# Two attention layers of a graph network: GpSimd's gathers written out, ScalarE's staging of indices dropped

## The chip, the cores and the metric

One NeuronCore of a Trainium2 chip runs the whole program. Its engines are TensorE (PE in the profile; its weight loads are PEld), VectorE (DVE), ScalarE (ACT), GpSimd (POOL) and SyncE (SP). The metric is the time of one execution on the device in microseconds (us). All tensors of a layer that don't fit on the chip lie in HBM.

## What is computed

Four layers of a graph network over 3,125 nodes with 128 features and 100,000 edges, each behind a layer norm and a ReLU, each added to its input. The two that matter here weigh edges by a softmax over the edges of a node:

```python
# layer 1: graph attention, 8 heads of 16
h = (x @ W).reshape(n, H, C)
e = leaky_relu(a_src[src] + a_dst[dst], 0.2)          # one score an edge and head
alpha = softmax of e over the edges with the same dst
out = segment_sum(h[src] * alpha, dst) + bias
...
# layer 3: queries of the sources against keys of the targets
scores = einsum('ehd,ehd->eh', q[src], k[tgt]) / 4
scores = (scores + edges @ We + be) * cons[tgt] + relu(distances @ Wd1 + bd1) @ Wd2 + bd2
weights = softmax of scores over the edges with the same tgt
out = segment_sum(weights * v[tgt], tgt) @ Wo + bo
```

Layer 0 is a polynomial of the graph's Laplacian, layer 2 three relational convolutions; the change doesn't touch them.

## The kernel before

The edges are sorted by target and dealt out to 816 tiles of 128 edges. `src_i` on the chip holds for every tile one column of 128 source numbers (one per partition). Both attention layers run the same function, `edge_rows`, over the tiles: G = 4 tiles are a group, R = 4 groups a step, so 204 groups in 51 steps. `R` is also the number of slots in each ring of buffers.

For group n, in slot r = n mod 4, five engines work side by side, each through its own instruction stream, tied together by semaphores:

- ScalarE (`scalar`) copies four columns of `src_i` into `st[:, slot, :]`, three groups ahead, once VectorE has consumed group n - 1 (line 2095 waits, line 2097 copies). In layer 3 it then picks 16 numbers for each tile of the next group (line 3203); in both layers it does the factors of a running sum once a step (lines 2429 to 2458), in layer 1 it also keeps blocks of pair sums (line 1947).
- GpSimd (`gpsimd`, line 2023) loops over the 51 steps. For each slot it waits for the staged indices, in layer 1 also for SyncE's store of the slot's last rows, and issues four indirect DMAs, the gathers (line 2031): tile g of the slot gets from HBM the rows of its 128 sources, 136 numbers a row in layer 1, 128 in layer 3.
- SyncE loads, 4 groups ahead, the targets' places within their window (line 2168), in layer 1 stores the gathered rows to HBM (line 2172) and once a step the results of the running sum (line 2464).
- VectorE makes one-hots from the places (line 2041), three groups ahead, and consumes group n (`consume`: layer 1 lines 2843 and 2844, layer 3 lines 3153 to 3167). The last instruction of `consume` raises `s_done`, which starts at R. In layer 3 VectorE multiplies the gathered rows by the keys and sums by head. In layer 1 it makes one-hots of the pair sums between (lines 1917 and 1919).
- TensorE turns one-hots into the targets' rows (line 2131) and, in layer 1, makes pair sums (line 1929).

Every engine's loop holds more than one group: VectorE's, ScalarE's and TensorE's hold two steps in layer 3 and more in layer 1, GpSimd's one step with 16 gathers. Nothing but the semaphores orders the engines among themselves; the order on each is the order of the code. Another stage, the first sort of the edges, issues 784 indirect DMAs from GpSimd (line 402, rows of 16 bytes, from the chip to HBM) that stand written out one behind the other.

## Time and profile before

| | us |
|---|---|
| median of 3 runs | 7,225.01 (7,213.89 to 7,237.66) |
| the profiled execution | 7,228.69 |
| its span, first to last instruction | 7,226.9 |
| layer 1's gathers, first to last | 2,421.4 to 3,777.9 |
| layer 3's gathers, first to last | 5,781.7 to 7,106.4 |

The profile has one line for each instruction that an engine executed, with its start, its duration, the idle time before it and what ended that idle time. Waits, branches and register instructions are not counted as busy; "issue" as a releaser means that the profile shows nothing that the engine waited for. Names leave out numbers: `l_edges_by_src` is the ring of gathered rows of either layer, and one can tell the layers apart by the source, `l_by_src` in layer 1 and `l_q` in layer 3. `l_edges_st` are the staged indices.

### The profile page before, as it was taken

What the parts mean: (1) busy time and instruction counts of PE and PEld (TensorE: products, weight loads), DVE (VectorE), ACT (ScalarE), POOL (GpSimd) and SP (SyncE); (2) the same over time, 40 slices, a digit from 0 to 9 for tenths busy, and PEclk for the clock granted to TensorE, in tenths of its full rate; (3) what the DMA queues carried; (4) which work ended last, traced back from release to release, by engine and by line L of the source; (5) the groups of instructions that cost most, each with busy time, mean ns of one, the idle gap of its engine ahead of it and who ended that gap; (6) DMA issues with size and microseconds to landing.
All of it is one profiled execution on the core that took longest, in us unless ns stands there. A gap on an engine that the chain in (4) does not pass through costs nothing. (4 is left out here: it accounts for less than half of the span.)

```text
span 7226.9 us, 87751 instructions
## 1 busy us (share of the span) xinstructions
PE 4193.4 (58%) x18024; PEld 2737.2 (38%) x18027; DVE 3135.0 (43%) x8308; ACT 917.6 (13%) x2931; POOL 3255.4 (45%) x3301
## 2 busy tenths in 40 slices
PE   6820111177799566667765658888888633333333
PEld 6700000022599333333334544444444322222232
DVE  6900111187796555545546761121121344444445
ACT  2100000011100121211210000010010022222221
POOL 0077777600000355555551005646546355555553
PEclk6555555588899787887777989898898855555555
DMA  4300000023477466666663546675665632222232
GB/s 125 94 2 13 8 2 2 10 64 100 156 257 262 126 170 164 168 167 165 172 169 86 145 136 230 216 245 204 213 238 204 198 73 66 69 68 68 67 68 55
DMA packets 564861, 910.88 MB, mean 126 GB/s; under 512 B 100563, under 2 KB 402664, under 8 KB 526004
## 3 DMA queue, kind: packets, MB, share of 16 engines
q1 hardware_dynamic: 459630, 742.44, 32.2%
q0 software_dynamic: 105024, 166.00, 10.1%
q8 instruction: 92, 1.51, 0.1%
q14 instruction: 115, 0.94, 0.0%
HBM read 677.34 MB, written 230.78 MB: 126 GB/s over the span
## 5 line engine op out<-in xcount | busy, mean ns | idle before, releaser
L2031 POOL DMA_INDIRECT l_edges_by_src<-l_by_src,l_edges_st x816 | 795.7, 975 | 1567.3 <-ACT l_edges_st L2080 1005.5
L3027 POOL DMA_INDIRECT l_gathered<-l_table,l_st x816 | 778.1, 954 | 1018.9 <-issue 829.2
L402 POOL DMA_INDIRECT by_src<-src_rec,src_pos x784 | 833.5, 1063 | 530.3 <-DVEq L315 290.6
L2031 POOL DMA_INDIRECT l_edges_by_src<-l_q,l_edges_st x816 | 781.9, 958 | 636.0 <-ACT l_edges_st L2097 300.0
L3096 PE MATMUL psum<-l_blocks,l_rows 128*128 128x512 f32 (+1 forms) x2016 | 891.2, 588 | 68.4 <-issue 65.4
L2131 PE MATMUL psum<-l_rows,l_edges_hot_t 128*128 x1632 | 423.7, 436 | 844.4 <-DVE l_scores L3167 533.3
L1929 PE MATMUL psum<-pair_hot_weight,pair_hot_dst 128*128 128x512 f32 x1200 | 719.3, 741 | 279.5 <-DVE pair_hot_dst L1919 181.8
L2131 PEld LDWEIGHTS psum<-l_rows,l_edges_hot_t 128*128 128x128 f32 x1632 | 360.9, 315 | 914.7 <-issue 914.6
L1163 PE MATMUL psum<-hot_block,hot_low_src 128*128 128x400 bf16 x1136 | 337.7, 420 | 594.6 <-issue 370.7
L3055 DVE TENSOR_SCALAR l_hot<-iota,l_loc,l_weight 128x128 f32<-128x128 f32 x816 | 224.1, 356 | 1051.7 <-DMA pair_blocks<-pair_block 222.4
L1135 DVE TENSOR_SCALAR hot_block<-block_iota,visit_key 128x400 bf16<-128x400 f16 x1136 | 281.3, 319 | 817.5 <-remote 357.4
L3096 PEld LDWEIGHTS psum<-l_blocks,l_rows 128*128 128x128 f32 x2016 | 385.6, 209 | 451.4 <-issue 446.5
L1929 PEld LDWEIGHTS psum<-pair_hot_weight,pair_hot_dst 128*128 128x128 f32 x1200 | 257.8, 233 | 570.8 <-issue 567.8
L1163 PEld LDWEIGHTS psum<-hot_block,hot_low_src 128*128 128x128 bf16 x1136 | 122.3, 108 | 814.5 <-issue 738.7
L2777 PE MATMUL psum<-l_scaled,l_counts 128*128 128x128 f32 x3750 | 425.7, 277 | 1.8 <-ACT l_scaled L2701 1.8
L2777 PEld LDWEIGHTS psum<-l_scaled,l_counts 128*128 128x128 f32 x3750 | 425.0, 194 | 1.9 <-issue 1.9
L1917 DVE TENSOR_SCALAR pair_hot_weight<-pair_iota,pair_staged 128x512 f32<-128x512 f32 x600 | 333.2, 555 | 159.6 <-PE psum L1929 60.2
L3107 PE MATMUL psum<-l_hot,l_gathered 128*128 128x128 f32 x1632 | 263.2, 305 | 163.9 <-issue 149.2
L2131 PEld LDWEIGHTS psum<-l_dst_rows,l_edges_hot_t 128*128 128x128 f32 x1632 | 244.1, 213 | 271.0 <-issue 270.4
L3107 PEld LDWEIGHTS psum<-l_hot,l_gathered 128*128 128x128 f32 x1632 | 241.7, 214 | 271.4 <-issue 271.2
L1626 PE MATMUL psum<-l_sum_rows,l_sum_hot 128*128 128x128 f32 x1632 | 251.0, 302 | 137.6 <-issue 123.9
L2131 PE MATMUL psum<-l_dst_rows,l_edges_hot_t 128*128 x1632 | 235.1, 272 | 132.3 <-issue 107.3
(563 smaller groups left out, 5288.8 us busy)
## 6 DMA issues: line engine op xcount, KB each, us to landing
l_blocks<-pair_blocks SPq DMA_DIRECT2D x216, 1024.0 KB
l_counts<-counts SPq DMA_DIRECT2D x67, 1600.0 KB, 7.0
pair_blocks<-pair_block SPq DMA_DIRECT2D x75, 1024.0 KB
l_edges_loc<-loc_by_tile SPq DMA_DIRECT2D x416, 128.0 KB
l_rows<-l_edges_by_src SPq DMA_DIRECT2D x204, 256.0 KB
l_sum_rows<-l_rows SPq DMA_DIRECT2D x204, 256.0 KB
counts<-count_rows SPq DMA_DIRECT2D x25, 1600.0 KB
attr_space<-in_edge_attr SPq DMA_DIRECT2D x14, 1568.0 KB
```

Source lines behind the costliest of these rows:

```text
L402: pool.indirect_dma_start(table, bass.IndirectOffsetOnAxis(ap=pos[:, e:e + 1], axis=0), rec[:, e, :], None).then_inc(s_out[g % R], 16)
L1135: v.tensor_scalar(self.hot_aj[:, h, n, :], self.at_aj[:, :, :].rearrange("p a j -> p (a j)"), self.key[:, bass.ds(m * TURN + (h * BATCH + ...
L1163: ins = pe.matmul(k.psum[:, bass.ds(bank * PSUM_BANK, AJ)], self.hot_s[:, h, n, :], self.hot_aj[:, h, n, :], start=False, stop=False)
L1626: ins = pe.matmul(k.psum[:, bass.ds(to[g] * D, D)], hot[:, r, g, :], rows[:, r, g, :], start=False, stop=False)
L1917: v.tensor_scalar(self.hot_w[:, place, :], self.wide[:, :], self.near[:, q, j, 1:2], self.near[:, q, j, 2:3], ALU.is_equal, ALU.mult).then ...
L1929: pe.matmul(self.bank(b), self.hot_d[:, place, :], self.hot_w[:, place, :], start=j == self.first[b], stop=j + 1 == self.first[b + 1]).the ...
L2031: pool.indirect_dma_start(a[:, r, g, :], None, table_src, bass.IndirectOffsetOnAxis(ap=st[:, r, g:g + 1], axis=0))\
L2131: ins = pe.matmul(by_place[:, q, g, 0:cols_dst], hot_t[:, r, g, :], by_dst[:, bass.ds(of[g], 1), :].rearrange("p a c -> p (a c)"), start=T ...
L2777: ins = pe.matmul(k.psum[:, to * D:(to + 1) * D], cnt[:, u, to * P:(to + 1) * P], scaled[:, r % 2, w, :], start=n == 0 and to == bank[0], ...
L3027: pool.indirect_dma_start(sent[:, p, g, :], None, by_type, bass.IndirectOffsetOnAxis(ap=st[:, p, g:g + 1], axis=0))\
L3096: ins = pe.matmul(k.ps[c][:, 0:n * P].rearrange("p (a s) -> p a s", s=P), rows[:, b, t * D:(t + 1) * D], blocks[:, 0:n, t, :], start=b == ...
L3107: ins = pe.matmul(k.psum[:, bass.ds(to[g] * P, P)], sent[:, p, g, :], hot[:, p, g, :], start=False, stop=False)
```

## The change

GpSimd's loop is replaced by 204 groups written out one behind the other. Each gather names its own column of `src_i`; the first R groups wait for nothing, and each later one waits for `s_done` to reach n + 1, which says that the group four back, the slot's last, has been consumed. In layer 1 the wait for the stored rows stays. The ring `st`, its semaphores and ScalarE's copies and the waits before them are gone.

```diff
-        st = k.sb(ctx, f"{tag}_st", [P, R, G], I32)
...
         def gpsimd(pool):
-            with pool.Fori(0, steps) as i:
-                for r in range(R):
-                    pool.wait_ge(s_st[r], i + 1)
+            for n in range(T // G):
+                i, r = divmod(n, R)
+                if i > 0:
+                    pool.wait_ge(s_done, n + 1)
                     if keep_rows is not None:
                         pool.wait_ge(s_kept[r], i * 16 + 1)
-                    pool.nop(nofuse=True)
-                    for g in range(G):
-                        pool.indirect_dma_start(a[:, r, g, :], None, table_src,
-                                                bass.IndirectOffsetOnAxis(ap=st[:, r, g:g + 1], axis=0))\
-                            .then_inc(s_row[r], 16)
+                for g in range(G):
+                    pool.indirect_dma_start(a[:, r, g, :], None, table_src,
+                                            bass.IndirectOffsetOnAxis(ap=k.src_i[:, n * G + g:n * G + g + 1], axis=0))\
+                        .then_inc(s_row[r], 16)
...
         def scalar(act):
-            for r in range(R - 1):
-                act.copy(st[:, r, :], k.src_i[:, r * G:(r + 1) * G]).then_inc(s_st[r], 1)
...
             def group(n, r, i, par, pair):
-                ahead = (r + R - 1) % R
...
-                act.wait_ge(s_done, n + R)
-                act.nop(nofuse=True)
-                act.copy(st[:, ahead, :], k.src_i[:, bass.ds((n + R - 1) * G, G)]).then_inc(s_st[ahead], 1)
```

GpSimd in layer 3, the whole loop before. The semaphores bear the names of their first users, since they are used again from stage to stage; here they are the four of the staged indices.

```order
L2024 UNCONDITIONAL_BRANCH
L2024 ISA
L2031 DMA l3_edges_by_src<-l3_q,l3_edges_st 128x128 [waits sort_low_v]
L2031 DMA l3_edges_by_src<-l3_q,l3_edges_st 128x128 x3
L2031 DMA l3_edges_by_src<-l3_q,l3_edges_st 128x128 [waits sort_low_one_set]
L2031 DMA l3_edges_by_src<-l3_q,l3_edges_st 128x128 x3
L2031 DMA l3_edges_by_src<-l3_q,l3_edges_st 128x128 [waits sort_low_counted]
L2031 DMA l3_edges_by_src<-l3_q,l3_edges_st 128x128 x3
L2031 DMA l3_edges_by_src<-l3_q,l3_edges_st 128x128 [waits sort_low_summed]
L2031 DMA l3_edges_by_src<-l3_q,l3_edges_st 128x128 x3
```

The same place after: the first 16 gathers, then the beginning of the 200 groups that follow. Here the semaphore is `s_done`.

```order
L2030 DMA l3_edges_by_src<-l3_q,src_i 128x128 x16
L2030 DMA l3_edges_by_src<-l3_q,src_i 128x128 [waits sort_dist_loaded]
L2030 DMA l3_edges_by_src<-l3_q,src_i 128x128 x3
L2030 DMA l3_edges_by_src<-l3_q,src_i 128x128 [waits sort_dist_loaded]
L2030 DMA l3_edges_by_src<-l3_q,src_i 128x128 x3
L2030 DMA l3_edges_by_src<-l3_q,src_i 128x128 [waits sort_dist_loaded]
L2030 DMA l3_edges_by_src<-l3_q,src_i 128x128 x3
```

The loop and its control instructions are gone, the wait has moved from ScalarE's semaphores to VectorE's, and 16 gathers have become 816 in the stream.

ScalarE in layer 3, from the last copy of a group's terms on, before (layer 3's first group in the loop):

```order
L3203 COPY l3_terms<-l3_terms_by_tile 128x16
L2095 REGISTER_ALU
L2097 ISA [waits sort_dist_loaded]
L2097 COPY l3_edges_st<-src_i 128x4
L2454 REGISTER_ALU
L2455 ISA [waits l1_score_steps]
L2458 COPY l3_run<-psum 128x16x8 [waits l1_turned_turned]
L2458 COPY l3_run<-psum 128x16x8
```

and after:

```order
L3196 COPY l3_terms<-l3_terms_by_tile 128x16
L2447 REGISTER_ALU
L2448 ISA [waits l1_score_steps]
L2451 COPY l3_run<-psum 128x16x8 [waits l1_turned_turned]
L2451 COPY l3_run<-psum 128x16x8
L2087 REGISTER_ALU
```

Between the picked terms and the copies of the running sum a register instruction, the wait for `s_done` and the staging copy are gone; this repeats in every group.

## Rows read from the trace of the kernel before

**Rows 1.** Busy time by stage, layers 1 and 3: stretch, length, busy us (instructions) of PE, PEld, DVE, ACT, POOL; clock, DMA.
```profile
2420.00:3790.00 1370.00, 944.14 (x3042) 512.12 (x3042) 686.63 (x2242) 269.74 (x804) 795.74 (x816) 0.78 0.61 166
5780.00:7110.00 1330.00, 462.89 (x1818) 389.02 (x1818) 563.54 (x1516) 302.80 (x1288) 781.87 (x816) 0.54 0.29 68
```

**Rows 2.** The page's groups: GpSimd's gathers of the two loops: busy, mean ns, idle before.
```profile
L2031 POOL DMA_INDIRECT l_edges_by_src<-l_by_src,l_edges_st x816 | 795.7, 975 | 1567.3 <-ACT l_edges_st L2080 1005.5
...
L2031 POOL DMA_INDIRECT l_edges_by_src<-l_q,l_edges_st x816 | 781.9, 958 | 636.0 <-ACT l_edges_st L2097 300.0
```

**Rows 3.** Waits in layer 1's loop: us in total, times, longest.
```profile
POOL l_edges_by_src L2031 <- ACT l_edges_st L2097: 317.9, 91, 6.4
```

**Rows 4.** Waits in layer 3's loop.
```profile
POOL l_edges_by_src L2031 <- ACT l_edges_st L2097: 300.0, 66, 7.5
...
DVE l_scores L3164 <- ACT l_terms L3203: 15.4, 6, 3.5
```

**Rows 5.** The gathers' line: durations, first and last start; then who waited for them.
```profile
L2031 POOL DMA_INDIRECT l_edges_by_src<-l_by_src,l_edges_st x816: 939/947/1275, 2421.4 to 3777.9; - x164
L2031 POOL DMA_INDIRECT l_edges_by_src<-l_q,l_edges_st x816: 941/947/1242, 5781.7 to 7106.4; - x164
...
who waited for it (us, times):
  DVE l_edges_by_src L3153: 3.2, 1
  DVE dst_f L2843: 1.5, 1
```

**Rows 6.** Timeline of GpSimd in layer 3: start, us, what, idle before and its releaser.
```profile
6379.10 0.95 POOL L2031 DMA_INDIRECT l_edges_by_src<-l_q,l_edges_st  x1 [2.74 <-ACT l_edges_st L2097]
...
6393.10 0.94 POOL L2031 DMA_INDIRECT l_edges_by_src<-l_q,l_edges_st  x1 [0.30 <-issue]
6395.17 0.94 POOL L2031 DMA_INDIRECT l_edges_by_src<-l_q,l_edges_st  x1 [1.12 <-issue]
...
6406.55 0.95 POOL L2031 DMA_INDIRECT l_edges_by_src<-l_q,l_edges_st  x1 [6.68 <-ACT l_edges_st L2097]
...
6420.53 0.94 POOL L2031 DMA_INDIRECT l_edges_by_src<-l_q,l_edges_st  x1 [0.30 <-issue]
6424.77 0.99 POOL L2031 DMA_INDIRECT l_edges_by_src<-l_q,l_edges_st  x1 [3.30 <-ACT l_edges_st L2097]
...
6444.12 0.95 POOL L2031 DMA_INDIRECT l_edges_by_src<-l_q,l_edges_st  x1 [4.58 <-ACT l_edges_st L2097]
```

**Rows 7.** Timeline of VectorE there: the last three instructions of groups.
```profile
6405.24 0.19 DVE L3167 TENSOR_TENSOR l_scores<-l_scores,l_terms 128x32 f32<-128x32 f32 x1
...
6410.31 0.19 DVE L3160 SCALAR_TENSOR_TENSOR l_scores<-l_scores,l_terms 128x32 f32<-128x32 f32 x1 [0.20 <-DVE l_scores L3156]
6410.61 0.19 DVE L3164 TENSOR_TENSOR l_scores<-l_scores,psum 128x32 f32<-128x32 f32 x1
6410.90 0.19 DVE L3167 TENSOR_TENSOR l_scores<-l_scores,l_terms 128x32 f32<-128x32 f32 x1
...
6416.70 0.19 DVE L3160 SCALAR_TENSOR_TENSOR l_scores<-l_scores,l_terms 128x32 f32<-128x32 f32 x1 [1.99 <-issue]
6418.83 0.19 DVE L3164 TENSOR_TENSOR l_scores<-l_scores,psum 128x32 f32<-128x32 f32 x1 [1.94 <-ACT l_terms L3203]
6421.66 0.19 DVE L3167 TENSOR_TENSOR l_scores<-l_scores,l_terms 128x32 f32<-128x32 f32 x1 [2.64 <-issue]
```

**Rows 8.** Timeline of ScalarE there: two staging copies.
```profile
6405.61 0.19 ACT L2097 COPY l_edges_st<-src_i 128x4 int32 x1 [1.43 <-DVE l_scores L3167]
...
6423.83 0.19 ACT L2097 COPY l_edges_st<-src_i 128x4 int32 x1 [2.66 <-issue]
```

**Rows 9.** Written-out scatters of an earlier stage, by stretch: length, POOL busy (instructions), clock, DMA.
```profile
400.00:600.00 200.00, 151.90 (x159) 0.50 0.03 2
...
900.00:1300.00 400.00, 312.88 (x286) 0.50 0.02 2
```

**Rows 10.** Timeline of TensorE's weight loads in that stage.
```profile
906.98 0.10 PEld L1163 LDWEIGHTS psum<-hot_block,hot_low_src 128*128 128x128 bf16 x1 [1.29 <-issue]
908.38 0.10 PEld L1163 LDWEIGHTS psum<-hot_block,hot_low_src 128*128 128x128 bf16 x1 [1.29 <-issue]
```

More of the change, by code:

```diff
@@ L1992, in edge_rows @@
         s_hot, s_mm, s_done = (k.sem(f"{tag}_{name}") for name in ("hot", "by_dst_made", "consumed"))
-        s_st, s_loc, s_kept = ([k.sem(f"{tag}_{name}{r}") for r in range(R)] for name in ("staged", "loc_loaded", "kept"))
+        s_loc, s_kept = ([k.sem(f"{tag}_{name}{r}") for r in range(R)] for name in ("loc_loaded", "kept"))
         s_row = k.pool_dma_sems(f"{tag}_gathered")
```

## The prediction

> **What bounds the kernel now.** I read four views in turn. First the busy time by stage [rows 1]: the edge loops of the two attention layers take some 1,360 and 1,325 of the 7,226.9 us of the span, and nothing else is touched. In the second, GpSimd is the busiest engine (781.87 us of 1,330); in the first TensorE is (944.14 of 1,370).
>
> Then the waits of GpSimd [rows 2 to 4]: it stood idle before its gathers for 317.9 us in 91 waits in layer 1 and for 300.0 us in 66 waits in layer 3, each ended by ScalarE's copy of four index columns. At first sight those 618 us are the prize. A gather takes 958 ns and its successor starts 0.30 us behind it, so 816 of them fill 1,027 of the 1,325 us.
>
> Third, who waits for the gathers [rows 5]: one instruction of VectorE in each layer, 3.2 and 1.5 us. The gathered rows are there long before they are used, in all 204 groups of a layer but these two. So a gather that starts earlier brings nothing by itself. What is late is the consumer.
>
> Fourth, the timelines show why the consumer is late. GpSimd's gathers come in unbroken runs [rows 6]: 12 from 6379.10, 4 from 6395.17, 12 from 6406.55, 12 from 6424.77. VectorE's last three instructions of a group start 0.30 us apart at 6410.3, but 2.1 and 2.8 us apart at 6416.7, although each still takes 0.19 us [rows 7]. ScalarE is slowed at the same time: its staging copy ends 0.4 us behind VectorE's consumption at 6405.43, but 2.2 us behind the one at 6421.85 [rows 7, 8]. Such a slow stretch begins about 5 us into a run and ends some 2 us behind its last gather: in it a group takes VectorE about 10.8 us (6411.1 to 6421.9) where three quick ones took 2.8 us each. I read this as: **while gathers have run unbroken for some 5 us, every other engine gets its instructions only slowly**. The loop's time is the time of gathering, in which the others crawl, plus the pauses of GpSimd, in which they catch up. What causes the slowness no row says, but it decides this change.
>
> **The change, part by part.**
> (1) ScalarE loses, for each group, a wait, one or two register instructions and the copy (0.19 us). That is 204 copies a layer, 39 us of an engine that is busy 303 us of 1,330 [rows 1, 8]. It also loses its tie to VectorE: the picking of layer 3's terms for the next group no longer stands behind a wait for the last group's consumption. VectorE's longest waits for these terms add up to 15.4 us, 6 times [rows 4], so I cost this at nothing; VectorE's own stream and, in layer 1, TensorE's cover it. If that cover were gone it would be a gain of some us.
> (2) GpSimd waits for VectorE's count itself. The ring condition is the same one (the group four back is consumed), only the relay is gone. A quick wait becomes 0.37 us shorter, a wait at the end of a slow stretch 2.2 us. By [rows 5] this is worth nothing on the path. It can't cost the wait itself: the wait sits on the first gather of a group as before, and only gathers queue behind it. In layer 1 the wait for SyncE's store of the slot stays as it was.
> (3) GpSimd's loop of 16 gathers becomes 816 instructions in a row. The loop's branch is taken while earlier gathers still run, so nothing is saved there: the spacing is the same 0.30 us inside and between turns. Whether a written-out gather is as quick as one in a loop is not shown for these loops, but another stage of this kernel has 784 of them written out [rows 9]. Between 400 and 600 us, when the rest is nearly idle, 159 fit in 200 us: 1.258 us each, the price in the loop. Between 900 and 1,300 us, with TensorE and VectorE in their loops, 286 fit in 400 us: **1.399 us each**. In that stretch TensorE's weight loads come 1.40 us apart, though each takes 0.10 us [rows 10], so it is the same slow condition. In the loops of the edge stages a gather keeps its pace in slow stretches too (in the run from 6406.55 the last of 12 starts 13.98 us behind the first, 1.27 us each) [rows 6]. The difference I take for the price of standing outside a loop while others are running.
>
> The bounds of that price: below, nothing (1.258 us as at 400 to 600); above, 1.399 us for all gathers. I take 1.399 for the gathers in slow stretches, since [rows 9] show it over 286 of them, and the present spacing for the others. In layer 3 that is 8 of the 12 of a run (all from 5 us on): 816 x 2/3 x (1.399 - 1.258) = 77 us. In layer 1 GpSimd waits more often (91 times against 66, so 9 gathers to a wait against 12) and its mean gather is 975 ns already (with 0.30 us between, 1.278) [rows 2]; I take a half: 816 x 1/2 x (1.399 - 1.278) = 49 us. Together gathering lasts **126 us longer**.
>
> What of it reaches the end? In added slow time the others do a quarter of the work of quick time (2.8 us against 10.8 us for a group), so three quarters are lost: **95 us**. GpSimd's pauses, some 300 us in each layer, would hide the longer gathering if they were slack; by the fourth view they aren't, because the others catch up in them.
> The sum, against the profiled execution (7,228.7 us, span 7,226.9): 7,228.7 + 95 = 7,324. The median of the runs is 3.7 us below that execution, so 7,320.
>
> The Trainium skill has a rule that speaks the other way ("Runtime: NRT & Kernel Launch", section "Instruction fetch mechanics"): engines stream their instructions in order ahead of use, a block's edge is mostly hidden, and a taken branch out of the window is what stalls, so kernels prefer to be written out. By it part (3) is free and the sum is 7,225. The trace agrees at 400 to 600 us (1.258 us) and disagrees at 900 to 1,300 (1.399 us).
>
> **The rivals.**
> *No change, 7,225.* Written-out gathers keep 1.25 us, say because the 1.399 us belongs to that stage's 16-byte scatters to HBM and not to their form. Then only earlier starts are left, which nobody waits for. For it: [rows 5], the 1.258 us, and the rule above. Against it: the same scatters ran at both prices, and what differed was whether others ran.
> *Faster, about 7,150.* The relay is on the path after all: each of the 157 waits gives back 0.37 us (58 us), and those at the end of a slow stretch 2.2 us; with a sixth of them of that kind, 157 x 1/6 x 1.8 = 47 us more, and a few us each from ScalarE's shorter stream, if the slow stretches are shorter for having fewer instructions in them. About 75 to 110 us. Against it: the rows wait ready for the consumer.
> *Slower by another way, 7,290 or, on top of the forecast, 7,380.* In layer 3 the pause is what lets the others recover, and a pause of 1.1 us does not do it: behind the one at 6394.04 the slow stretch went on. The pause before 6424.77 is 3.3 us now. It would be 1.1 us after the change, because VectorE was done at 6421.85. The turn with the short pause takes 27.45 us for 4 groups (6379.10 to 6406.55), 6.86 a group; the two with long pauses 37.57 us for 6 groups (6406.55 to 6444.12), 6.26. If half the groups of layer 3 go over to the first kind: 102 x 0.6 = 61 us. It decides where the pauses shrink below some 2 us.
>
> **How the numbers follow.** Forecast (gathers slowed by their form, 7,270 to 7,390): 0.40. Shrunken pauses, alone or on top: 0.15. No change: 0.22. Faster: 0.23. A measurement of this kernel can tell about 0.3%, 22 us, from no change, so faster 0.23, same 0.22, slower 0.55. The range goes from 7,165 (a small gain of the relay alone, 58 us) to 7,430 (near the upper bound of the gather's price, 816 x 2 x 0.13 = 212 us, all on the path); left out are the larger gains and both slow mechanisms in full.
>
> **What would show it.** Spacing of GpSimd's gathers in the edge loops: 1.40 us in the slow stretches if I am right, 1.25 if not. GpSimd's idle time before gathers in these loops falls from 618 us by more than half in every case; the question is whether the stages (1,357 and 1,325 us from the first gather to the last) [rows 5] get longer all the same. Pauses under 2 us in layer 3 with slow stretches running through them would show the third rival. VectorE waiting for gathered rows more than a few us would prove [rows 5] a bad guide. All other stages should stay within a few us. The forecast is wrong if the spacing stays at 1.25 us, or if it grows and the stages don't, which would mean that GpSimd's pauses were slack.

## The result: 2.3% faster, against the forecast

The changed kernel takes 7,057.2 us (median of 4 runs, 7,046.0 to 7,071.9); the kernel before 7,224.5 beside it (4 runs). The ratio is 0.977, 95% interval 0.975 to 0.979. The prediction said 7,320 us with a range of 7,165 to 7,430, and gave "slower" more than half of the chance. It was wrong in its sign.

The profiled execution has a span of 7,044.6 us, 182.3 less than before. GpSimd's gathers in the page's groups (line, engine, operation, what it writes and reads, count, then busy time, mean ns of one, idle time before and its releasers), which answer to [rows 2]:

```profile
L2030 POOL DMA_INDIRECT l_edges_by_src<-l_by_src,src_i x816 | 786.5, 964 | 1495.5 <-POOLq L1764 1002.5
...
L2030 POOL DMA_INDIRECT l_edges_by_src<-l_q,src_i x816 | 778.3, 954 | 563.4 <-DVE l_scores L3160 241.6
```

The same line by its durations, first and last start, and what it waited for and who for it, which answers to [rows 5]:

```profile
L2030 POOL DMA_INDIRECT l_edges_by_src<-l_by_src,src_i x816: 938/944/1208, 2417.0 to 3695.4; - x164
L2030 POOL DMA_INDIRECT l_edges_by_src<-l_q,src_i x816: 938/944/1175, 5680.4 to 6929.6; - x164
...
  issue: 464.7, 1461
  DVE l_scores L2837: 252.9, 92
  DVE l_scores L3160: 241.6, 73
...
who waited for it (us, times):
  DVE l_edges_by_src L3146: 0.3, 1
```

Three things are to be seen. A gather takes 944 ns (median) and the next starts 0.30 us behind it, as in the loop: the written-out gathers of this kernel do not have the price of 1.399 us. From first to last gather layer 1 takes 1,278.4 us (1,356.5 before) and layer 3 1,249.2 (1,324.7 before): together 153.6 of the 182.3 us. And the gain is idle time of GpSimd: it now waits for VectorE's consumption for 252.9 + 241.6 = 494.5 us in 165 waits, where it waited 617.9 us for ScalarE's copies in 157. The rest is in stages that the change doesn't touch, mostly between the two loops (2,003.7 us from layer 1's last gather to layer 3's first before, 1,985.0 now). That part is not the change's: of four kernels below that are the changed one up to layer 3, two took 1,987 and 1,989 us there (e15, e4) and two 2,004 and 2,005 (e11, e16). The profiled execution of the changed kernel is also among the quicker ones of its four (7,046.6 us against a median of 7,057.2), so the 167 us between the medians is the better measure of the gain.

The busy time by stage, layers 1 and 3 (stretch, length, busy us and instructions of PE, PEld, DVE, ACT, POOL, then clock and DMA), which answers to [rows 1], shows that no engine got less work but ScalarE:

```profile
2417.00:3710.00 1293.00, 963.21 (x3042) 520.82 (x3042) 694.97 (x2244) 244.43 (x596) 786.46 (x816) 0.79 0.64 177
...
5670.00:6940.00 1270.00, 467.05 (x1850) 393.76 (x1848) 579.60 (x1559) 271.06 (x1099) 778.33 (x816) 0.55 0.30 74
```

The timelines of GpSimd and of VectorE in layer 3 (start, us, what, idle time before and its releaser) show what a restart looks like now. They answer to [rows 6 to 8]:

```profile
6342.09 0.94 POOL L2030 DMA_INDIRECT l_edges_by_src<-l_q,src_i  x1 [2.81 <-DVE l_scores L3160]
...
6356.04 0.94 POOL L2030 DMA_INDIRECT l_edges_by_src<-l_q,src_i  x1 [0.31 <-issue]
6360.04 0.94 POOL L2030 DMA_INDIRECT l_edges_by_src<-l_q,src_i  x1 [3.06 <-DVE l_scores L3160]
```

```profile
6341.63 0.19 DVE L3160 TENSOR_TENSOR l_scores<-l_scores,l_terms 128x32 f32<-128x32 f32 x1 [1.24 <-issue]
...
6359.58 0.19 DVE L3160 TENSOR_TENSOR l_scores<-l_scores,l_terms 128x32 f32<-128x32 f32 x1
```

VectorE ends its last instruction of a group at 6341.82 and at 6359.77; the gathers start at 6342.09 and 6360.04, **0.27 us** behind. In the kernel before, VectorE ended at 6405.43, ScalarE's copy at 6405.80, and the gather started at 6406.55 [rows 6 to 8]: 0.37 us for the relay and another **0.75 us** from the copy to the gather. The prediction priced the first and did not see the second, although both ends of it stood in its rows.

### The profile page after: what moved, and what is told of

Read it like the earlier page. It is cut to its first block and busy times, and to the rows that moved or that the text cites. A ratio compares the mean times of both kernels' runs of the same rounds, so it can differ in the third digit from the quotient of the medians.

```text
span 7044.6 us, 85720 instructions
## 1 busy us (share of the span) xinstructions
PE 4200.1 (60%) x18026; PEld 2739.5 (39%) x18027; DVE 3150.8 (45%) x8308; ACT 856.9 (12%) x2517; POOL 3222.8 (46%) x3301
## 5 line engine op out<-in xcount | busy, mean ns | idle before, releaser
L2030 POOL DMA_INDIRECT l_edges_by_src<-l_by_src,src_i x816 | 786.5, 964 | 1495.5 <-POOLq L1764 1002.5
L402 POOL DMA_INDIRECT by_src<-src_rec,src_pos x784 | 815.6, 1040 | 546.7 <-DVEq L315 290.4
L2030 POOL DMA_INDIRECT l_edges_by_src<-l_q,src_i x816 | 778.3, 954 | 563.4 <-DVE l_scores L3160 241.6
```

Of the source, the lines that this page charges most:

```text
L402: pool.indirect_dma_start(table, bass.IndirectOffsetOnAxis(ap=pos[:, e:e + 1], axis=0), rec[:, e, :], None).then_inc(s_out[g % R], 16)
L2030: pool.indirect_dma_start(a[:, r, g, :], None, table_src, bass.IndirectOffsetOnAxis(ap=k.src_i[:, n * G + g:n * G + g + 1], axis=0))\
```

## Three theories, and the runs that tell them apart

Theory R: the relay through ScalarE was on the path, for the loop's time is that of gathering and of GpSimd's pauses. Theory F: the written-out form is what gained. Theory S: ScalarE's shorter stream did. All lengths of "loops" below go from the first gather to the last, layer 1 / layer 3. Five profiles of one and the same layer 1 (the changed kernel, and e4, e11, e15 and e16 below, which change nothing there) gave 1,278, 1,283, 1,303, 1,282 and 1,303 us, so differences under 25 us of one loop mean nothing. No two profiles of one and the same layer 3 were taken on a chip of this kind; its spread is taken to be like that. e11 and e15, alike but for one waiting instruction a group, differ by 49 us in all (7,163 and 7,114), so runs on different chips can lie further apart than their intervals say.

**e1, the form alone.** The kernel before with

```diff
-            with pool.Fori(0, steps) as i:
-                for r in range(R):
-                    pool.wait_ge(s_st[r], i + 1)
-                    pool.nop(nofuse=True)
+            for n in range(T // G):
+                i, r = divmod(n, R)
+                pool.wait_ge(s_st[r], i + 1)
                 ...
```

> The kernel before with one part of the change alone: GpSimd's gathers written out, 204 groups in a row, but each still waits for ScalarE's staged copy and takes its indices from it. Theory R (the relay through ScalarE is on the cycle of gathering and pausing, and that it is gone is the gain): no gain, 7,224 us, within 20 us; GpSimd's idle time in the two loops stays near 313 and 295 us. Theory F (the written-out form is the gain): near 7,060. If both count, in between.

Measured: 7,114.2 us, ratio 0.983 (0.982 to 0.985), with 7,231.5 for the kernel before on that chip; the loops 1,321 / 1,268. So 117 us, two thirds of the gain, come with the form, though ScalarE still relays. Theory R alone is refuted, and so is theory F alone, which said 7,060.

**e2, the relay alone.** The kernel before with a ring of eight staged groups, filled seven ahead, and

```diff
-                    pool.wait_ge(s_st[r], i + 1)
+                    pool.wait_ge(s_st[0], i * R + r + 1)
+                    pool.wait_ge(s_done, i * R + r + 1)
                     ...
                     pool.nop(nofuse=True)
```

> The kernel before with only the relay taken off GpSimd's path: GpSimd's gathers stay in a loop (of two steps, 32 gathers, and one step behind it), ScalarE makes exactly as many staging copies as before, but seven groups ahead into a ring of eight, and GpSimd itself waits for VectorE's count. Theory R: 7,060 to 7,085 us, GpSimd's idle time before gathers falls by some 140 us in the two loops together. Theory F (the written-out form is the gain) and theory S (ScalarE's shorter stream is the gain): near 7,224.

Measured: 7,205.0 us, ratio 0.995 (0.993 to 0.997); the loops 1,310 / 1,342. Layer 1 is 47 us shorter than before, layer 3 is not (18 us longer, within the spread). In layer 3 GpSimd's restarts came 0.74 us (median) behind VectorE's consumption, where it was 1.11 us before and is 0.27 in the changed kernel. Theory R had said 7,060 to 7,085: the relay alone is worth 0.5%, not 2%.

**e3, ScalarE's copies kept.** The changed kernel with its waits and copies put back into a ring that nobody reads:

```diff
+                act.wait_ge(s_done, n + R)
+                act.nop(nofuse=True)
+                act.copy(st[:, ahead, :], k.src_i[:, bass.ds((n + R - 1) * G, G)]).then_inc(s_st[ahead], 1)
```

> The changed kernel with ScalarE's waits for consumption and its 408 copies of indices put back, into a ring that nobody reads. Theory R: as the changed kernel, 7,057 us, within 15 us. Theory S (ScalarE's stream, freed of its wait for the last group's consumption, is the gain): near 7,224. A part of the gain lost would be ScalarE's part of it.

Measured: 7,082.9 us, ratio 0.9795 (0.978 to 0.981); the loops 1,295 / 1,255. ScalarE's part is the difference to the changed kernel, 0.3%, some 20 us. The two intervals touch (0.978 and 0.979), so it may also be nothing; theory S, which had the whole gain, is refuted.

```diff
                 if i > 0:
                     pool.wait_ge(s_done, n + 1)
+                    pool.nop(nofuse=True)
```

> The changed kernel with the waits of its written-out gathers carried by an instruction of their own in front of the group's first gather, as the loop before did it, instead of by that gather. Theory N (the gain of the form is that a gather which carries its own wait starts 0.27 us behind its releaser, one behind a separate waiting instruction 0.78 us; with some 190 waits in the two loops that is 95 us, and it is the form's whole gain): about 7,150 us, the loops longer by 45 to 55 us each. Theory L (what counts is that GpSimd no longer loops, the separate wait is free): 7,057.

This run came to a chip on which nothing of this exists (see "The other kind of chip"). Once more:

> The changed kernel with the waits of its written-out gathers carried by an instruction of their own in front of the group's first gather, once more, since on the chip of the last four runs the kernel before took 5,627 us and GpSimd never waited in the two loops. If the kernel before takes some 7,230 us here (GpSimd waits some 190 times in the two loops): theory N (a gather that carries its own wait starts 0.27 us behind its releaser, one behind a separate waiting instruction 0.78 us, and that is the form's whole gain): about 7,150 us; theory L (what counts is that GpSimd no longer loops): 7,057. If the kernel before takes some 5,630 us here: no difference, by either.

Measured: **7,252.6 us, ratio 1.004 (1.003 to 1.006)**: one waiting instruction a group takes back the whole gain and some 30 us more. GpSimd doesn't loop here and ScalarE doesn't relay, so neither is the gain by itself, and theory L is refuted. Layer 1 took 1,330 us, 27 to 51 more than the five profiles without the `nop`; theory N had said 45 to 55. Layer 3 took 1,374, 125 us more, far over the 45 to 55 of theory N, and that is why the whole lies 100 us above its 7,150. So the waiting instruction's own half us explains layer 1; in layer 3 it also changed the pattern, which the next section takes up. GpSimd's line:

```profile
L2031 POOL DMA_INDIRECT l_edges_by_src<-l_by_src,src_i x816: 942/947/1245, 2420.2 to 3749.9; - x164
L2031 POOL DMA_INDIRECT l_edges_by_src<-l_q,src_i x816: 942/947/1184, 5750.9 to 7125.1; - x164
...
  DVE l_scores L3161: 343.6, 65
  DVE l_scores L2838: 302.8, 91
```

## Layer 3: pauses that are too short

What happened in layer 3 is the prediction's third rival. I counted in each trace GpSimd's pauses, those over which a slow stretch (register instructions of 0.70 us on the other engines) went on, and the time for a group in cycles with one run and in cycles of several:

| kernel | loop 3, us | restart behind consumption, us | pauses, slow stretch goes on over | us a group: one run / several |
|---|---|---|---|---|
| changed | 1,249 | 0.27 | 74, 4 | 6.14 / 6.11 |
| e3 copies kept | 1,255 | 0.27 | 78, 9 | 6.08 / 6.61 |
| e1 form alone | 1,268 | 0.65 | 75, 10 | 6.22 / 6.34 |
| e4 early release | 1,302 | -0.71 | 80, 18 | 6.38 / 6.42 |
| before | 1,325 | 1.11 | 76, 10 | 6.46 / 6.76 |
| e2 relay alone | 1,342 | 0.74 | 98, 36 | 6.29 / 6.73 |
| e9 wait apart | 1,374 | 0.75 | 97, 43 | 6.66 / 6.80 |

(The expectations say 2 for the changed kernel; a full count gives 4. These counts move by one or two with how far apart two such instructions may lie in one stretch.) The restart's delay (median) doesn't order the loops by itself.

How long a pause has to be, the traces say: over the seven kernels the slow stretch went on over about 130 of the 140 pauses under 2 us and over 6 of the 438 longer ones. That is layer 3. In layer 1 pauses don't decide it: there the slow stretch went on over some 35 of 114 pauses in the changed kernel and some 14 of 107 in the kernel before, and the changed one is 78 us shorter all the same.

In e9, GpSimd gathers 12, stops for half a us to 2 us, gathers 4 more within the slow stretch, and then waits some 6 us; it does so 43 times. In the rows below it stops for 0.52 us, and the separate wait alone holds it, since VectorE had ended at 6331.98, before the 12th gather had. GpSimd's waits and VectorE's last instructions of groups in e9's layer 3:

```profile
6317.45 0.95 POOL L2031 DMA_INDIRECT l_edges_by_src<-l_q,src_i  x1 [6.16 <-DVE l_scores L3161]
...
6332.73 0.94 POOL L2031 DMA_INDIRECT l_edges_by_src<-l_q,src_i  x1 [0.52 <-issue]
...
6344.56 0.94 POOL L2031 DMA_INDIRECT l_edges_by_src<-l_q,src_i  x1 [7.14 <-DVE l_scores L3161]
```

```profile
6316.51 0.19 DVE L3161 TENSOR_TENSOR l_scores<-l_scores,l_terms 128x32 f32<-128x32 f32 x1
...
6319.38 0.19 DVE L3161 TENSOR_TENSOR l_scores<-l_scores,l_terms 128x32 f32<-128x32 f32 x1
...
6322.18 0.19 DVE L3161 TENSOR_TENSOR l_scores<-l_scores,l_terms 128x32 f32<-128x32 f32 x1
...
6331.79 0.19 DVE L3161 TENSOR_TENSOR l_scores<-l_scores,l_terms 128x32 f32<-128x32 f32 x1 [2.63 <-issue]
...
6343.62 0.19 DVE L3161 TENSOR_TENSOR l_scores<-l_scores,l_terms 128x32 f32<-128x32 f32 x1
```

Behind the first of these, two groups quickly, the third after 9.6 us, the fourth after 11.8: 27.1 us for four groups. The changed kernel's runs of 12 have a pause of 3.1 us (mean of 38) and cycle in 18.0 us, 6.0 a group; its 19 cycles of 8 take 6.0 a group too, its 10 cycles of 16 take 6.6. Two runs ask whether the pause's length decides.

**e4, the slot given back earlier** (in the changed kernel, layer 3 only; `s_c` counts VectorE's three steps of a group, and the first is the sum by head, behind which the rows are free):

```diff
-                    pool.wait_ge(s_done, n + 1)
+                    pool.wait_ge(s_c, 3 * (n - R) + 1)
```

> The changed kernel, in layer 3 with the slot of gathered rows given back earlier: GpSimd waits for the sum by head, the last of VectorE's instructions that reads the rows, not for the last of the three small ones behind it. In the changed kernel those three end 0.98 us later (median), over 3 us in 57 groups; GpSimd's waits could start up to 156 us earlier in sum. Theory R, taken to its end (every us that GpSimd waits less is a us of the loop): layer 3's loop 1,250 -> about 1,095 us, 6,900 in all. Theory P (VectorE needs GpSimd's pauses to catch up in, so from here on shorter pauses only come more often): no gain or a loss, 7,050 to 7,120. In between would say how much of the pauses is needed.

Measured: 7,120.5 us, ratio 0.985 (0.984 to 0.987), with layer 3 at 1,302 us, 53 more than in the changed kernel. Restarts came 0.71 us *ahead* of the end of consumption (median), and GpSimd's wait for VectorE did not fall but rose, from 241.6 to 283 us. Up to 156 us seemed to be had, and the loop got slower. So a us of a wait is not a us of the loop, and theory R is refuted here. Theory P named the result (7,050 to 7,120, no gain or a loss), but its way is only half shown: 18 pauses, not 4, left the slow stretch on, yet the cycles with such a pause cost hardly more than e4's others (6.42 against 6.38 us a group), and those others are slower than the changed kernel's (6.14). What makes them so no run tells.

**e10, longer pauses.** The other way round, with e9 as its base, in layer 3 only. (Its first form, on e2's base, also came to the chip without slow stretches.)

> The kernel with the relay alone taken away, with one more wait for GpSimd in layer 3: for the one-hots of the group that it is about to gather for, which VectorE makes directly behind the consumption that frees the slot. It makes each restart 0.6 us later when instructions come quickly and some 3 us later within a slow stretch. In the kernel with the relay alone 36 of 98 pauses in layer 3 were too short to end the slow stretch (of the changed kernel's 74 pauses: 2), and layer 3 took 1,343 us against 1,325 before, although its waits ended earlier. Theory P (a pause that is over before the slow stretch ends costs more than it gives): layer 3 gets shorter in spite of the later restarts, 1,270 to 1,310 us. Theory R (every us of a wait is a us of the loop): it gets longer by 30 us or more.

```diff
                     pool.wait_ge(s_done, n + 1)
+                    pool.wait_ge(s_hot, n + 1)
                     pool.nop(nofuse=True)
```

> The changed kernel with its waits carried by an instruction of their own (7,253 us; layer 3's loop 1,375 us, 43 of 97 pauses there over before the slow stretch ends, 6.80 us a group in those cycles), and in layer 3 with one more wait for each group: for the one-hots that VectorE makes directly behind the consumption that frees the slot. Every restart comes later by this, 0.6 us when instructions come quickly and up to 3 us within a slow stretch. If the kernel before takes some 7,230 us here: theory P (a pause that is over before the slow stretch ends costs more than it gives): layer 3 gets shorter by 40 to 100 us although its restarts come later, 7,150 to 7,210 in all, and few pauses leave the slow stretch on. Theory R (every us of a wait is a us of the loop): layer 3 longer by 40 us or more, above 7,290. If the kernel before takes some 5,630 us here: no difference, by either.

Measured: 7,224.2 us, ratio 0.9986 (0.998 to 0.9996), just above theory P's 7,210. Layer 3 took 1,345 us, 29 less than e9, although every restart waits for one more thing and starts 2.8 to 3.4 us behind the consumption (47 of 54 restarts). The slow stretch went on over 4 of 55 pauses, not 43 of 97. The two ratios, 1.004 (1.003 to 1.006) for e9 and 0.9986, lie apart, so theory R is refuted for this pattern by its direction; its size is below what P expected, since GpSimd now ran 16 gathers and paused 6.7 us (45 times, 6.6 us a group, the price that a run of 16 has in the changed kernel too). With 4 short pauses and 1,345 us, e10 also shows that few short pauses don't make a quick loop. So the pattern costs, and its cure costs too. Why the changed kernel falls into cycles of 12 and e9 into 12 and 4 I can't derive: half a us decides it.

## What slows the others: gathering without a break, on some chips

**One gather of four.** The changed kernel with, in layer 3,

```diff
-                for g in range(G):
+                for g in range(G if i == 0 or pick is None else 1):
```

and the product replaced by a maximum (e7, e13 and e16 are one kernel).

> The changed kernel with three of the four gathers of every group of layer 3 left out from the fifth group on, and the product of rows and keys replaced by their maximum (same instruction, other operation), so its output is not the reference's. Theory I and every other that has the others crawl under unbroken gathering: no slow stretches in layer 3's loop, and the loop at VectorE's quick pace of 2.8 to 3.2 us a group, about 650 us instead of 1,250. If the slowness is not GpSimd's doing: the 0.70 us instructions stay and the loop stays above 1,000 us.

> The changed kernel with three of the four gathers of every group of layer 3 left out from the fifth group on, and the product of rows and keys replaced by their maximum, so its output is not the reference's; once more, for a chip on which the kernel before takes some 7,230 us. If it is unbroken gathering that slows the others: no slow stretches in layer 3's loop, which then takes 700 to 760 us, as on the chip on which the kernel before took 5,627 us (722 us). If the slowness of this chip has another cause: instructions of 0.70 us stay and the loop takes above 900 us.

> The changed kernel with three of the four gathers of every group of layer 3 left out from the fifth group on, and the product of rows and keys replaced by their maximum, so its output is not the reference's; for a chip on which the kernel before takes some 7,230 us. If it is unbroken gathering that slows the others: hardly a slow stretch in layer 3's loop, which then takes 700 to 760 us (722 us on the other kind of chip). If the slowness has another cause: instructions of 0.70 us stay and the loop takes above 900 us.

The third came to a chip like the first one (7,225 us for the kernel before) and gave 6,577.7 us. Its layer 3 took 732 us instead of 1,249, with one slow stretch of 20 us in the loop instead of 797 us of them (register instructions of 0.70 us, counted in the traces):

```profile
L2030 POOL DMA_INDIRECT l_edges_by_src<-l_q,src_i x216: 943/947/1062, 5728.3 to 6459.9; - x108
```

So the prediction's reading is shown: it is GpSimd's unbroken gathering that slows the others there. The run takes away three quarters of the gathers and of what they transfer together, so it doesn't tell the issuing from the transfers. The prediction's words were that the others get their instructions only slowly. Whatever slows them, it is not the fetching of instructions from memory: in layer 3's loop of the kernel before, with over 800 us of slow stretches, the DMA queues of instructions moved three pieces (packets, MB, share of 16 engines' time):

```profile
q8 instruction: 1, 0.02, 0.0%
q14 instruction: 2, 0.02, 0.0%
```

**The other kind of chip.** The first two of these runs, and five more, came to two chips on which the kernel before takes 5,627 and 5,636 us. There layer 3's loop has no slow stretch. The changed kernel was run on one of them:

> The changed kernel itself, beside the two above on the same chip. If the kernel before takes some 7,230 us here: 7,057 us within 15. If it takes some 5,630 us: no difference, since GpSimd gathers without a pause in both loops there.

GpSimd gathers without a pause in either loop, 1,035 / 1,028 us, and now VectorE waits for gathered rows:

```profile
L2030 POOL DMA_INDIRECT l_edges_by_src<-l_by_src,src_i x816: 940/946/1232, 1663.2 to 2698.5; - x164
L2030 POOL DMA_INDIRECT l_edges_by_src<-l_q,src_i x816: 940/945/1206, 4500.3 to 5528.2; - x164
...
who waited for it (us, times):
  DVE l_edges_by_src L3146: 221.2, 124
  DVE dst_f L2836: 54.6, 37
```

The change is worth **nothing there**: 5,645.2 against 5,636.0 us, ratio 1.002 (0.9997 to 1.004). e5 (0.999), e6 (0.9996), e8 (1.000) and e12 (0.998) give the same, and e7 and e13, with one gather of four, take layer 3's loop to 722 us, as e16 does on the first kind (732). What differs between the chips no trace says. On the first kind, four chips in the experiments gave 7,221 to 7,234 us for the kernel before. The changed kernel itself was timed on one chip of each kind, so its 2.3% rests on four runs of one chip; its layer 1 was repeated on the chips of e4, e11, e15 and e16 and gave 1,282 to 1,303 us.

## Shorter streams for the others: an attempt at a better kernel

In a slow stretch each register instruction of an engine takes 0.70 us, so the next idea was to have fewer. The changed kernel with

```diff
             if pairs is None:
-                with engine.Fori(0, steps // 2) as j:
-                    ...
+                for i in range(steps):
+                    for r in range(R):
+                        body(i * R + r, r, i, i % 2, None)
                 return
```

> The changed kernel with VectorE's, ScalarE's and TensorE's loops of layer 3 written out as well (SyncE's stays a loop). Their waits then stand against constants: of VectorE's 23 instructions a group 8 register ones go. Theory I (in the slow stretches every instruction of an engine takes its turn of 0.70 us, so what counts is how many an engine has to get through): a group in a slow stretch takes 7 us instead of 10.8, GpSimd waits less, layer 3's loop 1,250 -> 1,050 to 1,150 us, about 6,900 in all. Theory M (the slow stretches come from how fast new instructions arrive, and a loop of two steps is spared that, so written-out streams are slow all the time): layer 3 longer than 1,250 us.

> The changed kernel with VectorE's, ScalarE's and TensorE's loops of layer 3 written out as well, once more, for a chip on which the kernel before takes some 7,230 us. Theory I (in the slow stretches every instruction of an engine takes its turn of 0.70 us, so what counts is how many an engine has to get through; of VectorE's 23 a group 8 register ones go): layer 3's loop 1,250 -> 1,050 to 1,150 us, 6,860 to 6,960 in all. Theory M (a loop of two steps is served better than a stream that is new all the time): layer 3 longer than 1,250 us, 7,080 or more. If the kernel before takes some 5,630 us here: no difference, by either.

The second, on a chip of the first kind: 7,163.5 us, ratio 0.991 (0.989 to 0.9925). Layer 3 took 1,312 us, 63 more than in the changed kernel. Theory I's 1,050 to 1,150 is refuted; theory M had the direction, though not the way. VectorE's waits in e11's layer 3 (line, what ended the wait, us in total, times, longest):

```profile
DVE l_edges_by_src L3142 <- remote: 432.6, 60, 12.3
DVE l_scores L3149 <- ACT l_terms L3192: 77.4, 15, 8.3
```

VectorE is not slow instruction by instruction any more. It stands still instead, for up to 12 us at a time, before its product of rows and keys, and goes on some 3.4 us (median) behind the end of GpSimd's last gather. "remote" names nobody. Is it the gathered rows? I split the wait in two:

```diff
                 v.wait_ge(s_mm, n + 2)
+                v.nop(nofuse=True)
                 v.wait_ge(s_row[r], (i + 1) * (16 * G))
                 v.nop(nofuse=True)
```

> The kernel with the loops of layer 3 written out on four engines (7,163 us), its VectorE waiting for the targets' rows and for the gathered rows by two instructions one behind the other instead of one. In that kernel VectorE stood idle for 432.6 us in 60 waits before its product of rows and keys, each until some 3.7 us behind the end of GpSimd's run, and the profile names nothing that it waited for. Theory A (the gathered rows are told to VectorE only once GpSimd's run has ended): the second of the two instructions, the wait for gathered rows, holds those idle times. Theory T (it is TensorE's rows): the first holds them. If the kernel before takes some 5,630 us here: neither lasts, and rows are used within 3 us of their last gather.

> Once more, for a chip on which the kernel before takes some 7,230 us: the kernel with the loops of layer 3 written out on four engines, VectorE waiting for the targets' rows and for the gathered rows by two instructions. Theory A (the gathered rows are told to VectorE only once GpSimd's run has ended): the second of the two, the wait for gathered rows, holds some 430 us of VectorE's idle time in layer 3. Theory T (it is TensorE's rows): the first holds it.

e12 was on a chip of the other kind and shows no such standstill (5,628 us). e15 was on one of the first kind: 7,114.3 us, ratio 0.985 (0.982 to 0.988), layer 3 1,304 us. The standstill is there, 512.7 us of it:

```profile
DVE l_edges_by_src L3144 <- remote: 512.7, 60, 13.0
```

One of them in VectorE's timeline, and GpSimd's gathers beside it:

```profile
6124.74 0.46 DVE L2036 TENSOR_SCALAR l_edges_hot_t<-l_edges_loc,pid 128x512 f32<-128x512 bf16 x1
6136.05 0.69 DVE L3144 TENSOR_TENSOR l_edges_by_src<-l_edges_by_src,psum 128x512 f32<-128x512 f32 x1 [10.85 <-remote]
```

```profile
6113.04 0.94 POOL L2026 DMA_INDIRECT l_edges_by_src<-l_q,src_i  x1 [6.03 <-DVE l_scores L3158]
...
6131.86 0.94 POOL L2026 DMA_INDIRECT l_edges_by_src<-l_q,src_i  x1 [0.30 <-issue]
```

By their durations neither wait holds it. The first of the two, over all 204 groups (min/median/max ns):

```profile
L2052 DVEq EVENT_SEMAPHORE  x204: 21/21/21, 5691.7 to 6995.9; - x102
```

But these durations don't tell whether VectorE waited. The wait behind the product, which is over only when the product's 0.69 us are, shows 21 ns 204 times as well, for its record begins only 39 ns (median) behind the product's end:

```profile
L3146 DVEq EVENT_SEMAPHORE  x204: 21/21/21, 5692.9 to 6997.4; - x102
```

The times at which the semaphores rise do tell. In this standstill TensorE's semaphore (`s_mm`, the targets' rows are made) rose at 6135.89, and the first wait's record begins at 6135.92. In all 60 waits put down to "remote" the record begins 26 to 28 ns behind such a rise, and in e11's 60 it is 27 to 29 ns. The semaphore of the gathered rows had last risen at 6118.83, 17 us earlier (8.7 us or more in each of the 71 waits over 1 us). So theory T holds, the first wait is the one that lasts, and theory A is refuted.

TensorE's matmuls for these rows, however, are recorded long before:

```profile
6120.10 2.17 PE L2122 MATMUL psum<-l_rows,l_edges_hot_t 128*128 x8
...
6123.19 2.18 PE L2122 MATMUL psum<-l_rows,l_edges_hot_t 128*128 x8 [0.91 <-issue]
```

The one that raises the semaphore ended at 6122.28 (ends of matmuls are modelled), 13.6 us before the rise, and the next group's rise came late with it, at 6136.02. Over the 60 waits the rise came 13.6 us (median) behind the matmul's end, in e11 13.0. On the other kind of chip (e12, e14) it comes within 0.1 us in all 204 groups; in e15 it does in 59. What holds it back under gathering no record shows. It is not that instructions have to be fetched: 13 of the 60 waits have a transfer of an instruction queue in them, the other 47 have none. Whether the 0.70 us of the register instructions have the same cause stays open.

The Trainium skill ("Runtime: NRT & Kernel Launch", section "Instruction fetch mechanics") has instructions streamed ahead at a cost that is mostly hidden, and kernels better off written out. The traces agree with the first: on the other kind of chip the written-out loops cost nothing (e6, ratio 0.9996), and on the first kind most standstills go without a fetch. The second they don't bear out there: the kernel with more written out lost to the changed one by 106 us (e11) and 57 us (e15), with 433 and 513 us of VectorE's waits for the late semaphore.

None of the kernels tried beats the changed one on the first kind of chip.

## Why the prediction was wrong, step by step

*"What bounds the kernel now"* held in the main. Unbroken gathering slows the others (e16: one gather of four, layer 3 from 1,249 to 732 us), though not by keeping fetched instructions from them, nobody waits long for rows, and loops take the time of gathering plus pauses. The conclusion from it, that an earlier gather brings nothing, doesn't follow from it and was the first error: if a loop's time is gathering plus pauses, and the other engines have room in the quick first 5 us of a run, a shorter pause is time won. That is the sentence "By [rows 5] this is worth nothing on the path" in part (2). [rows 5] say who waits for rows. The question was who waits for GpSimd to begin, and that was GpSimd itself, for 618 us [rows 3, 4].

*Part (1), ScalarE, costed at nothing* (a gain of some us without cover): 0.3%, some 20 us at most, by e3 against the changed kernel. Small, and rightly called.

*Part (2)* said that the wait sits on the first gather of a group as before. It did not: before, it sat on an instruction of its own. The order printed ahead of the prediction shows the wait at the first gather in both kernels, and this is what misled me; the trace had it, 0.75 us between the copy's end at 6405.80 and the gather at 6406.55 [rows 6, 8], against the 0.27 us of a gather that carries its wait. e1 (87 us less of it, loops 92 us shorter) and e9 (put back, gain gone) show this as the largest single term. In e9's layer 1 it is worth about its own length (27 to 51 us for 91 waits of half a us); in layer 3 e9 loses 125 us, of which its length explains some 50 and the rest goes with the changed pattern of runs.

*Part (3)*, 1.399 us for a written-out gather in slow stretches, was wrong outright. Within runs they start 1.27 / 1.26 us apart (means, 1.28 / 1.26 before), in slow stretches too: the first of the 12 at 6342.09 and the last at 6356.04 are 13.95 us apart. So the 1.399 us of [rows 9] belongs to that stage, as the rival "no change" had it. I took a difference between two stretches of one stage and carried it into another. The 126 us of longer gathering and the 95 us from it are all void.

*The rival "faster", 7,150*, was the right mechanism for the part that it saw. Its sum, 157 x 0.37 + 47 = 105 us, with the 0.5 us of the waiting instruction added for each of the 157 waits, would have been 105 + 79 = 184; the loops gave 154 and the kernel 167. Its term for a restart was mis-sized at 0.37 us where the rows had 0.37 + 0.75, of which 0.27 remains.

*The rival "slower by another way"*, shrunken pauses, is real as a pattern: e4 is 53 us longer in layer 3 than the changed kernel, e9 125, of which the later starts explain some 50, and e2's layer 3 gained nothing from its earlier restarts. That the short pauses themselves are the whole cost is not shown (e4, e10). It didn't strike in the changed kernel, which has 4 such pauses. The point from which I let it decide, pauses under some 2 us, fits layer 3: about 130 of 140 pauses under 2 us left the slow stretch on, 6 of 438 longer ones did, and in e9 the pauses behind runs of 12 are 1.3 us (mean), in the changed kernel 3.1.

## What to carry to other kernels

Ask of a wait not only who waits for its result, but whether the waiting engine's pauses are a part of the cycle. In a ring whose producer stands still while the consumer frees a slot, each half us between "freed" and "started again" can be paid once a pause (in layer 1 here; in layer 3 the pattern of runs counted for more), and where the wait is carried (by the working instruction, or by one of its own in front) was worth more here than the relay through another engine. And a gain or a loss that comes from how engines disturb each other can be there on one chip and absent on the next: 2.3% on one kind of chip here, nothing on the other. When a profile shows a short duration for a waiting instruction, that alone doesn't say that nothing was waited for: look at when the semaphore rose.

## What I had not expected of the hardware

- The kernel before took 7,221 to 7,234 us on four chips and 5,627 and 5,636 us on two others, with the same DMA traffic. On the latter no slow stretch lasts over 10 us in the whole program, none is in layer 3's loop, and GpSimd with all its gathers never pauses in the edge loops.
- A gather that carries its own wait starts 0.27 us behind its releaser; one behind a separate waiting instruction, 0.75 to 0.78 us (medians).
- On the first kind of chip, VectorE with a written-out stream is not slowed instruction by instruction under gathering but stands still for up to 13 us, until TensorE's semaphore rises, 13.6 us (median) behind the recorded end of the matmul that raises it; on the other kind it rises within 0.1 us. With a loop of two steps VectorE's register instructions and waits take 0.70 us each in the same stretches.
- In layer 3, pauses of GpSimd under 2 us left the slow stretch on (about 130 of 140), longer ones ended it (432 of 438).
